# Reading the moving operands of projections and value products in an interleaved column order

## What is computed

```python
xn = layernorm(x)                                   # x: (8, 1024, 256)
q = (xn @ Wq + bq) + pe                             # 8 heads of 128
k, v = split(xn @ Wkv + bkv); k = k + pe            # one head, shared
attn = softmax(causal(q @ k.T / sqrt(128))) @ v     # (8, 1024, 8 * 128)
attn = attn @ Wo
xr, xk = mixes of xn and xn shifted by one token
ffn = sigmoid(xr @ W_r.T) * (relu(xk @ W_k.T) ** 2 @ W_v.T)
out = x + attn + ffn
```

## Time and profile before

| what | value |
|---|---|
| median of 3 runs | 1506.69 us (1505.67 to 1507.88) |
| the profiled execution's own time | 1506.69 us |
| its span in the trace | 1504.9 us |
| PE, share of the span busy | 99% |
| PEld | 96% |
| VectorE (DVE) | 84% |
| GpSimd (POOL) | 75% |
| ScalarE (ACT) | 71% |

### The profile page before, as it was taken

How to read it: one execution, slowest core, us unless ns; L and a number is a source line. 1 busy time by engine, 2 the same in 40 slices (tenths; PEclk the granted TensorE clock), 3 DMA queues, 4 the chain that set the end, 5 groups by cost and what they waited for, 6 DMA issues and landing times.

```text
span 1504.9 us, 36254 instructions
## 1 busy us (share of the span) xinstructions
PE 1482.6 (99%) x11724; PEld 1448.2 (96%) x11724; DVE 1268.4 (84%) x3424; ACT 1068.0 (71%) x2563; POOL 1128.9 (75%) x1541
## 2 busy tenths in 40 slices
PE   7999999999999999999999999999999999999998
PEld 7999999999999999999999999999999999999998
DVE  6999878898788987998879888798977888789885
ACT  6777667776677767767677776776767777677764
POOL 6687777777777877777777776777777787777875
PEclk8999999999999999999999999999999999999999
DMA  4144422444224442244423444134441344403453
GB/s 129 48 131 129 142 75 64 134 125 147 72 65 133 135 134 68 83 120 137 134 60 88 127 128 144 46 98 128 134 141 34 113 131 138 136 27 108 119 157 105
DMA packets 225801, 164.39 MB, mean 109 GB/s; under 512 B 51792, under 2 KB 220880, under 8 KB 225616
## 3 DMA queue, kind: packets, MB, share of 16 engines
q1 hardware_dynamic: 224768, 161.69, 35.6%
q10 hardware_dynamic: 848, 0.40, 0.1%
HBM read 81.27 MB, written 77.59 MB: 106 GB/s over the span
## 4 chain that ended last, share of the span: by engine, by line
PE 81%; DVE 10%; issue 4%; POOL 3%; DMA 1%; ACT 1%; SPq 0%; DVEq 0%; POOLq 0%; ACTq 0%
PE pS L1040 27%; PE pO L1181 22%; PE pG L1040 13%; PE pG L1127 9%; PE pT L1143 8%; DVE X L1019 2%; DVE pt L943 1%; DVE Y L923 1%; DVE kt L831 1%; POOL X L571 1%; DVE xn L808 1%; DMA park_dram<-Y 1%; DVE mix L860 1%; POOL qt L527 1%; DVE qtmp L849 1%
## 5 line engine op out<-in xcount | busy, mean ns | idle before, releaser
L764 ACT ACTIVATE X<-X,bias 128x16 f32<-128x16 f32 (+56 forms) x512 | 376.1, 734 | 150.7 <-DVE bias L1019 149.0
L1040 PE MATMUL pS<-kt,qt 128*128 128x288 f32 (+41 forms) x2304 | 460.1, 329 | 4.5 <-DVE bias L1019 3.4
L571 POOL TENSOR_SCALAR X<-X,rec 128x16 f32<-128x16 f32 (+56 forms) x512 | 378.2, 739 | 44.2 <-DVE rec L913 33.4
L1040 PEld LDWEIGHTS pS<-kt,qt 128*128 128x128 f32 x2304 | 365.7, 189 | 17.1 <-issue 5.3
L546 POOL TENSOR_TENSOR pt<-pt 128x256 fp32r<-128x256 f32 (+5 forms) x192 | 316.6, 1649 | 60.3 <-ACT pt L686 59.8
L1181 PE MATMUL pO<-pt,v 128*128 128x256 f32 x2192 | 307.6, 284 | 1.2 <-DVE ot L998 0.9
L1019 DVE CUSTOM_DVE_ANT_1 X<-pS,mask 128x528 f32<-128x528 f32 (+31 forms) x256 | 245.6, 959 | 47.1 <-PE pS L1040 42.3
L1181 PEld LDWEIGHTS pO<-pt,v 128*128 128x128 f32 x2192 | 271.9, 189 | 2.6 <-DVE ot L998 2.1
L943 DVE TENSOR_TENSOR pt<-pt,pT 128x512 fp32r<-128x512 f32 (+3 forms) x440 | 207.6, 493 | 35.1 <-ACT pt L692 32.2
L757 ACT CAST ot<-pO 128x256 fp32r<-128x256 f32 x256 | 95.5, 373 | 184.0 <-PE pO L1181 117.8
L692 ACT CAST pt<-pT 128x512 fp32r<-128x512 f32 (+3 forms) x448 | 188.0, 450 | 30.8 <-PE pT L1143 30.5
(11 more groups left out here) (120 smaller groups left out, 2298.6 us busy)
## 6 DMA issues: line engine op xcount, KB each, us to landing
park_dram<-Y SPq DMA_DIRECT2D x32, 512.0 KB, 2.6
pt<-park_dram SPq DMA_DIRECT2D x128, 128.0 KB, 2.8
park_dram<-Y SPq DMA_DIRECT2D x32, 448.0 KB, 3.0
pt<-park_dram SPq DMA_DIRECT2D x128, 112.0 KB, 2.5
park_dram<-Y SPq DMA_DIRECT2D x32, 384.0 KB, 2.9
pt<-park_dram SPq DMA_DIRECT2D x128, 96.0 KB, 2.3
park_dram<-Y SPq DMA_DIRECT2D x32, 320.0 KB, 2.7
pt<-park_dram SPq DMA_DIRECT2D x128, 80.0 KB, 2.1
```

The costliest lines, as they stand in the source:

```text
L571: nc.gpsimd.tensor_scalar(x_row(s, 0, w), x_row(s, 0, w), rec[:, j:j + 1], sign(s), ALU.mult, ALU.mult).then_inc(normed, 1)
L764: nc.scalar.activation(x_row(s, 0, w), x_row(s, 0, w), ACT.Exp, bias=bias[:, j:j + 1], scale=-1.0, accum_out=total[:, j:j + 1]).then_inc(e ...
L1040: last = nc.tensor.matmul(out, a[i], m[j], start=start and k == 0, stop=stop and k == n - 1)
```

## The change

A view `woven` is put on the moving operand and on the output of some matmuls. It reads the 256 columns in pieces of 16 (64 bytes): first piece of the first half, first piece of the second half, second piece of the first half, and so on. The output view has the same order, so each column lands where it did. The number of instructions, the columns in each, the order of the instructions, all waits and all other engines are as before. It is put on Q, KV, FK, FR, FV and WO, and on the value products with the high part of `pt`. The scores (L1040, moving `kt`), the transposes and the value products with the low part of `pt` (stationary `vn`) stay as they are. `turns_of(part)` is 0 or 1 for every step here, so `flat` is always true.

```diff
+LINE = 16
...
+        def woven(ap):
+
+            return ap.rearrange("p (y x n) -> p x y n", y=2, n=LINE)
...
-                        last = product(out[:, i * CHUNK:(i + 1) * CHUNK],
+                        last = product(woven(out[:, i * CHUNK:(i + 1) * CHUNK]),
                                        [([w[:, ct, i * D:(i + 1) * D] for w in wkv],
-                                         [x[:, ct, :] for x in xt]) for ct in range(CT)])
+                                         [woven(x[:, ct, :]) for x in xt]) for ct in range(CT)])
...
-                        last = product(out[:, t * E:(t + 1) * E],
+                        last = product(woven(out[:, t * E:(t + 1) * E]),
                                        [([m[:, ct, t * P:(t + 1) * P] for m in mh],
-                                         [w[:, ct, :] for w in wr]) for ct in range(CT)])
+                                         [woven(w[:, ct, :]) for w in wr]) for ct in range(CT)])
...
-                            last = nc.tensor.matmul(out[:, 0:E], ot[i][:, h, :], wo[j][:, h, :],
+                            last = nc.tensor.matmul(woven(out[:, 0:E]), ot[i][:, h, :], woven(wo[j][:, h, :]),
                                                     start=(i, j, h) == (0, 0, 0), stop=i == 1 and h == H - 1)
...
-                    summed = pO[:, 0:2 * P].rearrange("p (t a c) -> p t a c", t=2, a=4)
+                    flat = turns_of(part) != 2
+                    in_runs = pO[:, 0:2 * P].rearrange("p (t a c) -> p t a c", t=2, a=4)
+                    in_order = woven(pO[:, 0:2 * P]) if flat else in_runs
+
+                    def high(k):
+                        if flat:
+                            return woven(pt[0][:, pair_no(b, part) % 2, k * 2 * P:(k + 1) * 2 * P])
+                        return pt_of(0, b, part)[:, :, :, k, :]
+
...
-                        last = nc.tensor.matmul(summed, (vn if j else v[i])[:, k, :],
-                                                pt_of(j, b, part)[:, :, :, k, :],
+                        last = nc.tensor.matmul(in_runs if j else in_order, (vn if j else v[i])[:, k, :],
+                                                pt_of(1, b, part)[:, :, :, k, :] if j else high(k),
                                                 start=n == 0, stop=n == 3 * nk - 1)
...
-                            last = nc.tensor.matmul(summed, vs[:, part // H % TPC, :],
-                                                    pt_of(0, b, part)[:, :, :, nk - 1, :],
+                            last = nc.tensor.matmul(in_order, vs[:, part // H % TPC, :], high(nk - 1),
                                                     start=False, stop=True)
```

More of the change, by code:

```diff
@@ L1105, in fill @@
                     for j in range(CT):
-                        last = product(out[:, j * CHUNK:(j + 1) * CHUNK],
+                        last = product(woven(out[:, j * CHUNK:(j + 1) * CHUNK]),
                                        [([w[:, ct, j * P:(j + 1) * P] for w in wk],
-                                         [m[:, ct, :] for m in mh]) for ct in range(CT)])
+                                         [woven(m[:, ct, :]) for m in mh]) for ct in range(CT)])
                 elif kind == "FR":
@@ L1117, in fill @@
                     for t in range(TPC):
-                        last = product(out[:, t * E:(t + 1) * E],
+                        last = product(woven(out[:, t * E:(t + 1) * E]),
                                        [([m[:, ct, t * P:(t + 1) * P] for m in kh],
-                                         [w[:, ct, :] for w in wv]) for ct in range(CT)])
+                                         [woven(w[:, ct, :]) for w in wv]) for ct in range(CT)])
                 elif kind == "WO":
```

## The result

| | median us | runs |
|---|---|---|
| before | 1506.18 | 1502.03 to 1507.88, 4 runs |
| changed | 1533.22 | 1529.94 to 1534.87, 4 runs |

The changed kernel takes 1.0184 times as long, with a 95% interval of 1.0167 to 1.0201: 27 us slower, where 14.5 us faster was forecast, and above the range that ended at 1528. The profiled execution of it took 1529.94 us, the lowest of its runs, with a span of 1528.2; before, these were 1506.69 and 1504.9.

A forecast was written before the change was run, and what follows sets the result against it. TensorE was taken to bound the kernel; 6856 woven matmuls going from 115.5 to 113.0 ns save 17.1 us, of which 0.85, 14.5 us, arrive: 1506.7 to 1492 us. Range 1470 to 1528 us, likeliest case 1484 to 1498.

The forecast's parts named there:

- What bounds the kernel: Whole kernel: TensorE, busy 99% of the span at full clock, sets the time, so a matmul's pace reaches the end nearly in full.
- The pace before: Matmuls to be woven: mean distance between starts taken as 115.5 ns, between two steady paces of about 113 and 118.
- The number that it was multiplied by: Count of woven matmuls, 6856, each to save 115.5 - 113.0 ns, 17.1 us of TensorE time.
- the first reading of the surplus: In each matmul, 6 to 11 ns come from the moving stream and next weights' load interfering at certain addresses.
- nothing meets, and every woven matmul should be at the better pace: Woven stream and weight load stay 64 bytes apart, so woven matmuls run at 113 ns; 1486 to 1492 us, chance 0.46.
- the score matmuls' surplus: Score matmuls of 512 columns: 233 ns against 213.3, 19 ns over, of which a weight load covers at most half.
- A jump as such does not forbid it: Seven low-part products in runs of 32 columns have 116.5 ns, less than FR without jumps, so 113 stays possible.
- slower, by the jumps in the read: Rival: each break in the read's address order costs; woven matmuls at 118.0 ns, 17.1 us more, 1524 us, chance 0.18.
- Slower, by the jumps in the write: Rival: each piece written to PSUM costs 0.86 ns; pace 127, loss 79 us, 1586 us, chance 0.10.
- The two read ports: TensorE's ports for moving operand and weight load are independent, so nothing to avoid; rival of no effect, 1507 us, chance 0.14.
- How much arrives: At the kernel's end: 0.85 of TensorE's saving counts, by its chain share, so 14.5 of 17.1 us.

The follow-up runs named there:

- e4_no_gap: The kernel before without the 64 bytes between wo and wq, so moving and stationary operands start at the same offset: 1525.63 us, 1.0142 times before.
- e2_write_only: The changed kernel with moving operands read side by side again, only outputs written in pieces of 16: 1506.07 us, 1.0003 times before.
- e1_read_only: The changed kernel with outputs written side by side again, only moving operands read in pieces of 16: 1532.81 us, 1.0189 times before.
- e6_pieces_32: The changed kernel with pieces of 32 columns in place of 16, read and write alike: 1519.12 us, 1.0096 times before.
- e7_values_only: The changed kernel with only the value products woven and all projections side by side: 1509.94 us, 1.0029 times before.

## Why the prediction was wrong, point by point

**What bounds the kernel** held: TensorE's pace alone changed, and in the traces the span grew by what it adds up to, 23.3 us for 23.5.

**The pace before** held: 115.5 was taken from cut rows and busy times, 115.99 is the mean of all distances. The number that it was multiplied by didn't: of the 6856 matmuls only 5664 have a distance at that pace in front of them, and the others, at the heads of groups, didn't change measurably.

**The step that failed** is the first reading of the surplus. That the pace depends on the addresses of both operands was right for columns side by side: the offset alone is worth 20.8 us in e4_no_gap, and FR's 118.1 is close to the 117.8 that matmuls alone have at FR's offset. That the stream and the load meet is still an argument. The wrong step was "nothing meets, and every woven matmul should be at the better pace": 113.0 ns was forecast, and 120.15 measured. It assumed that the stream runs as fast in pieces as side by side. It doesn't: at 512 columns and equal offsets it takes 240.0 against 226.7 ns, and at 256 columns pieces of 16 have 120.0 at every offset, so no distance between stream and load helps them. Whether the stream alone loses this or the stream with a load beside it stays open. I had a row for the doubt, the score matmuls' surplus that a load can't explain, and drew from it only that the better pace was not to be beaten, not that a stream in pieces of 64 bytes could have a price of its own. (The "some 6%" there isn't worked out: that row gives 19 of 213 ns, 9%. The 6% is what the best pace of 512 columns, 226.7 ns, has.)

**"A jump as such does not forbid it"** rested on one low-part group of seven at 116.5 ns. Pieces of 32 are in truth the milder case (118.7 in the halves-by-turns order, between 113.3 and 120.0), and one group of seven is neither the pace of its kind nor a bound for pieces half as long. The mean of its kind, 118.0, was the nearest row, and it stood above the 115.5 to beat: read without the theory, it forecast a loss.

**The rival "slower, by the jumps in the read"** named the mechanism, on the side of the read, and was given 0.18. Its term was mis-sized: 118.0 ns from pieces of 32, where pieces of 16 have 120.15. That is 2.5 ns where 4.16 were measured, partly made up by the count that was too large: 17.1 us against 23.5 in the traces and 27.0 in the medians. So 1524 us against 1533, and the range, which was built on it, ended too low. Its mechanism needs a correction: breaks that leave pieces of 64 columns or more cost nothing, pieces of 32 and less do.

**"Slower, by the jumps in the write"** is refuted by e2_write_only, 1.0003 times before. The Trainium skill's page "Advanced Engine Details and Errata" has two sentences on it under "PSUM Cachelines", as the prediction says; for pieces of 16 columns this run refutes the first and fits the second.

**The two read ports.** The Trainium skill, page "SBUF — State Buffer", section "Who interferes with whom", calls the port of the moving operand and that of the weight load independent. That alone doesn't cover what the runs show: at 256 columns side by side the pace depends on the offset between the two operands, 113.3 to 120.0 ns.

**How much arrives**: 0.85 of a gain was assumed, all of a loss. From before to after, to e1_read_only, e4_no_gap, e6_pieces_32 and e7_values_only the distances within groups grew by 23.5, 24.0, 20.5, 16.9 and 7.0 us, and the medians by 27.0, 28.0, 20.8, 14.3 and 4.7. So a loss arrives in full to within some 4 us, on either side. The kernel before alone varies by as much from one execution to the next (1502.03 to 1507.88), so no part that waits absorb is shown. What share of a gain would arrive, no run tests.

## What to carry to other kernels

A kernel bound by float32r matmuls of 256 columns gains or loses by addresses alone, 1.4% here. Let the weights start 64 bytes further than the moving operand, modulo 256 bytes, and read the moving operand in pieces of 64 columns or more. With 384 and 512 columns equal offsets were better than 64 bytes. The order of writing into PSUM was free down to pieces of 16 columns. Before an access order is changed throughout a kernel, price it in a kernel of matmuls alone, where ten orders cost one run.

## What the runs showed of the hardware

- A stream of 512 float32r columns side by side takes 226.7 ns at best, 13.3 ns more than its columns at 2.4 GHz; with its halves by turns in pieces of 32, 16, 8 and 4 columns it takes 236.7, 240.0, 243.3 and 250.0.
- With 256 columns the offset between the operands gives 113.3 to 120.0 ns, and 0 and 64 bytes gave the same as 256 and 320. With more columns, of the two offsets tried, the other one is better: 226.7 at equal offsets and 233.3 at 64 bytes for 512 columns, 173.3 and 176.7 for 384.
- At 64 bytes the same kind of group runs steadily at 113.3 or at 117.8 ns, in the kernel with the very same tensors too. What in the entry decides was not found. A way to enter always at 113.3 would be worth 5664 x 2.7 = 15 us here, an estimate from the mean of 115.99 ns.
